# Graph attention in duos: one stretch of scores and one of contexts for two graphs

## The reference

```python
h = maximum(layernorm(x), 0)
q, k, v = heads(h @ Wq + bq), heads(h @ Wk + bk), heads(h @ Wv + bv)
scores = einsum('bhqd,bhkd->bhqk', q, k) / sqrt(64)
probs = softmax(scores + where(adj, 0, -9e15), axis=-1)
ctx = einsum('bhqk,bhkd->bhqd', probs, v)
out = x + (merge_heads(ctx) @ Wf + bf)
```

## Time and profile before

| what | value |
|---|---|
| median of three runs | 1001.98 us (1000.74 to 1003.02) |
| the profiled execution | 1000.85 us |
| its span in the trace | 999.0 us |
| granted TensorE clock, mean | 0.991 of full speed |

### The profile page before, as it was taken

One profiled execution on the slowest core, in us unless ns is written; L12 is line 12 of the kernel. 1 busy time (PEld: TensorE's weight loads), 2 busy tenths in 40 slices (PEclk: granted clock), 3 DMA queues, 4 the chain that ended last, 5 costly groups with the idle time before them and its releaser, 6 DMA issues.

```text
span 999.0 us, 28223 instructions
## 1 busy us (share of the span) xinstructions
PE 948.1 (95%) x8649; PEld 510.8 (51%) x8649; DVE 838.4 (84%) x1621; ACT 780.8 (78%) x2373; POOL 670.3 (67%) x1163
## 2 busy tenths in 40 slices
PE   1889999999999999999999999999999999999976
PEld 0445555555555555555555555555555555555543
DVE  4688888888888888898888888888889888888774
ACT  3687788888878888888888887888888888888663
POOL 4676677777776767767777677776776777777431
PEclk9999999999999999999999999999999999999997
DMA  7447656566566565655656656656565565666454
GB/s 199 75 90 152 123 126 141 127 139 147 130 135 136 129 140 130 148 133 126 141 127 141 145 130 133 138 129 139 132 148 133 124 143 128 140 146 121 92 94 90
DMA packets 359834, 130.86 MB, mean 131 GB/s; under 512 B 325376, under 2 KB 359808, under 8 KB 359808
## 3 DMA queue, kind: packets, MB, share of 16 engines
q1 hardware_dynamic: 359808, 130.54, 60.4%
HBM read 29.82 MB, written 25.17 MB: 55 GB/s over the span
## 4 chain that ended last, share of the span: by engine, by line
issue 44%; POOL 41%; PE 5%; ACT 2%; POOLq 2%; DVE 2%; DMA 2%; SPq 0%; DVEq 0%; ACTq 0%
POOL x_bias L807 13%; POOL s L816 11%; POOL rstd L775 7%; POOL mask L786 3%; POOL shift L778 2%; POOL rstd L770 2%; PE ps_qk L301 2%; POOL shift L772 2%; DMA pt<-parts 2%; POOL h_parts L795 1%; POOLq L165 1%; PE ps_v L301 1%; PE ps_r L301 1%; ACT s L473 1%; DVE s L650 1%
## 5 line engine op out<-in xcount | busy, mean ns | idle before, releaser
L473 ACT ACTIVATE s<-s,neg_max 128x128 f32<-128x128 f32 x768 | 297.7, 390 | 53.3 <-DVE neg_max L664 53.3
L816 POOL TENSOR_TENSOR s<-s,inv_sums 128x384 f32<-128x384 f32 x256 | 212.2, 829 | 132.7 <-DVE inv_sums L639 132.7
L795 POOL TENSOR_TENSOR h_parts<-h,h_parts 128x384 f16<-128x384 f32 x128 | 121.3, 948 | 146.1 <-ACT h_parts L515 146.1
L301 PE MATMUL ps_v<-w_hi_v,ht 128*128 128x384 f16 x768 | 209.4, 328 | 0.0
L301 PE MATMUL ps_qk<-ht,w_hi_q 128*128 128x512 f16 x576 | 172.5, 381 | 3.6 <-DVE w_lo_q L545 3.3
L301 PE MATMUL ps_qk<-ht,w_hi_k 128*128 128x512 f16 x576 | 171.3, 379 | 0.0
L807 POOL TENSOR_TENSOR x_bias<-x_in,out_bias 128x384 f32<-128x384 f32 x128 | 170.1, 1329 | 0.4
L494 ACT ACTIVATE parts<-s 128x768 f16<-128x768 f32 x128 | 107.3, 838 | 55.0 <-POOL s L816 55.0
L650 DVE SCALAR_TENSOR_TENSOR s<-ps_s,unscale,mask 128x384 f32<-128x384 f32 x256 | 145.2, 609 | 1.0
L473 ACT ACTIVATION_READ_ACCUMULATOR s<-s,neg_max 128x1 f32 x768 | 145.5, 189 | 0.0
L301 PE MATMUL ps_r<-w_hi_f,ct_hi 128*128 128x384 f16 x384 | 128.2, 334 | 14.3 <-DVE ct_lo L688 13.1
(11 more groups left out here) (77 smaller groups left out, 1806.6 us busy)
## 6 DMA issues: line engine op xcount, KB each, us to landing
x_in<-in_x SPq DMA_DIRECT2D x128, 192.0 KB, 2.9
out<-y SPq DMA_DIRECT2D x128, 192.0 KB, 2.1
ht<-h_parts SPq DMA_TRANSPOSE x128, 2.9
adj_in<-in_adj SPq DMA_DIRECT2D x32, 64.0 KB, 2.7
pt<-parts SPq DMA_TRANSPOSE x128, 3.7
w_raw_f<-in_L_gnn_Wf SPq DMA_DIRECT2D x1, 576.0 KB, 5.2
w_raw_q<-in_L_gnn_Wq SPq DMA_DIRECT2D x1, 576.0 KB, 6.2
w_raw_v<-in_L_gnn_Wv SPq DMA_DIRECT2D x1, 576.0 KB, 7.3
```

The source lines that it names most:

```text
L301: last = mm(psum, parts_a[a](i), parts_b[b](i), start=n == 0, stop=n == len(todo) - 1)
L473: last = activation(s[:, b, hd, :], s[:, b, hd, :], ACT.Exp, bias=neg_max[:, b, hd:hd + 1], accum_out=sums[:, b, hd:hd + 1])
L795: nc.gpsimd.tensor_tensor(h_parts[:, b, 1, :], h[:, b, :], h_parts[:, b, 0, :], ALU.subtract).then_inc(h_lo_ready, 1)
L816: nc.gpsimd.tensor_tensor(s[:, b, half, :], s[:, b, half, :], inv_sums[:, b, half].unsqueeze(2).to_broadcast([128, PAIRS, NODES]), ALU.mul ...
```

## The change

The unit of a slot becomes a duo, two graphs, 0 and 1. A slot of TensorE now has three tiles, the values of duo t+1, the projections of duo t-3, the scores of duo t and the contexts of duo t-2:

```diff
-                scores(t, k)
-                projection(t - 3)
-                qk_tile(tiles[0])
-                context(t - 2, k - 2)
-                v_tile()
-                if two:
-                    qk_tile(tiles[1])
+                qk_tile(0)
+                qk_tile(1)
+                projection(0)
+                values(0)
+                qk_tile(2)
+                values(1)
+                projection(1)
+                scores(0)
+                scores(1)
+                context(1)
+                context(0)
```

PSUM is divided anew: four banks for the scores of two graphs, two for tiles, and two that values, projections and contexts share (`ps_m`):

```diff
-        ps_s = ps("ps_s", [128, 2, 512])
+        ps_s = ps("ps_s", [128, 2, 2, 512])
         ps_qk = [ps(f"ps_qk{i}", [128, COLS]) for i in range(2)]
-        ps_c = ps("ps_c", [128, 512])
-        ps_r = ps("ps_r", [128, 512])
-        ps_v = [ps(f"ps_v{i}", [128, 512]) for i in range(2)]
+        ps_m = ps("ps_m", [128, 2, 512])
```

On the shared banks `projection(0)` and `values(0)` wait for the remainder of the contexts (`ct_lo_ready`), `values(1)` for `residual(0)` (`y_ready`), `projection(1)` for `lower_v(0)` (`v_ready`), `context(1)` for `lower_v(1)` and `context(0)` for `residual(1)`. The order of ScalarE in a slot becomes:

```diff
+                upper_context()
+                norm(0)
+                qk_upper(0)
+                upper_probs(1)
+                exponentials(0, 0)
+                qk_upper(1)
+                exponentials(0, 1)
+                v_upper(0)
+                exponentials(1, 0)
+                qk_upper(2)
+                v_upper(1)
+                upper_probs(0)
+                norm(1)
+                exponentials(1, 1)
+                upper_h()
```

That of VectorE:

```diff
+                masked_scores(0)
+                lower_context()
+                maxima(0)
+                qk_lower(0)
+                lower_probs(1)
+                masked_scores(1)
+                maxima(1)
+                residual(0)
+                qk_lower(1)
+                spread()
+                lower_v(0)
+                spread_done()
+                reciprocals(0)
+                mean_and_variance()
+                qk_lower(2)
+                lower_v(1)
+                residual(1)
+                lower_probs(0)
+                reciprocals(1)
```

And that of GpSimd:

```diff
                 factors()
-                mask_of_next()
+                normalised(1)
                 lower_h()
                 biased_x()
+                wait_for_mask()
                 normalised(0)
-                normalised(1)
+                mask_of()
```

Instructions that become wider: the masked scores, the reciprocals and `normalised` take all six heads of a graph at once; `lower_h`, `upper_h`, `biased_x`, `upper_context`, `lower_context`, the mask and the factors take both graphs of a duo at once. `lower_probs` keeps its 768 columns:

```diff
+                def lower_probs(i):
+                    u = t - (1, 2)[i]
...
+                    wait(dve, parts_hi, 2 * u + 1 + i)
+                    tt(parts[:, i, 1, :], s[:, i, :, :].rearrange("p h n -> p (h n)"), parts[:, i, 0, :],
                        ALU.subtract).then_inc(parts_lo, 1)
...
+                def masked_scores(i):
+                    u = t - 1
...
+                    wait(dve, scores_ps, 2 * u + 1 + i)
+                    wait(dve, mask_ready, u + 1)
+                    wait(dve, parts_lo, 2 * u - 1 + i)
...
                 def biased_x():
-                    u, r = t + XB, (k + XB) % RING
+                    u, r = t - 1, (k - 1) % RING
...
+                    wait(pool, xr_loaded[r], 4 * (u - r) + 16)
+                    nc.gpsimd.tensor_tensor(x_res[:, r, :, :], x_res[:, r, :, :],
+                                            out_bias[:, :].unsqueeze(1).to_broadcast([128, 2, FEAT]), ALU.add
                                             ).then_inc(xb_ready, 1)
```

x is loaded twice: once for the layer norm seven duos ahead (`x_in`, one DMA per graph), and again into `x_res` (one DMA per duo) for the residual sum. SyncE's order in a slot:

```diff
+                if valid(t + LOAD):
+                    u, r = t + LOAD, (k + LOAD) % RING
...
+                        wait(sp, parts_lo, 2 * t - 3)
+                    sp.dma_start(x_in[:, r, 0, :], x_rows[:, bass.ds(2 * u, 1), :].rearrange("n g f -> n (g f)")
...
+                    sp.dma_start_transpose(pt[:, k % 2, 0, :, :], parts[:, 0, :, :].rearrange("p a n -> p (a n)")
...
+                        wait(sp, h_lo_ready, t + TURN + 1)
+                    sp.dma_start(x_in[:, r, 1, :], x_rows[:, bass.ds(2 * u + 1, 1), :].rearrange("n g f -> n (g f)")
...
+                    sp.dma_start_transpose(ht[:, ((k + TURN) % RING) // 2, (k + TURN) % 2, :, :].rearrange("p a (g n) -> p (a g) n", g=2),
+                                           h_parts[:, b, :, :].rearrange("p a n -> p (a n)")).then_inc(h_turned[b], 16)
...
+                        wait(sp, parts_lo, 2 * t - 2)
+                    sp.dma_start(x_res[:, k, :, :], x_rows[:, bass.ds(2 * t, 2), :]).then_inc(xr_loaded[k], 16)
...
+                    sp.dma_start_transpose(pt[:, k % 2, 1, :, :], parts[:, 1, :, :].rearrange("p a n -> p (a n)")
...
+                        wait(sp, y_ready, 2 * u + 1 + i)
+                        sp.dma_start(out_rows[:, bass.ds(2 * u + i, 1), :].rearrange("n g f -> n (g f)"), y[:, i, :]
...
+                    sp.dma_start(adj_in[:, at, :, :], adj_rows[:, bass.ds(2 * t + GROUP, GROUP), :]
```

More of the change, by code:

```diff
@@ L174, in slots @@
                 for i in range(RING):
-                    slot(base + i, FIRST + i)
-            for t in range(LOOP_END, GRAPHS + LATE):
+                    slot(base + i, i)
+            for t in range(LOOP_END, DUOS + LATE):
                 slot(t, t % RING)
[L179 to L186, removed]
-        TILE = [(0, 0), (1, 0), (1, 1), (0, 1), (1, 2), (0, 2)]
[L191 to L199, removed]
+        TILE = [(0, 0), (1, 0), (1, 1), (0, 1), (1, 2), (0, 2)]
         x_rows = x.rearrange("g n f -> n g f")
@@ L323, in slot, with qk_tile @@
             def slot(t, k):
[L324 to L331, removed]
+                static = isinstance(t, int)
+                def qk_tile(i):
+                    if not valid(t + AHEAD):
+                        return
+                    tile = 3 * (k % 2) + i
+                    wn, pair = "qk"[TILE[tile][0]], TILE[tile][1]
+                    group, at = 1 - k // 2, slice(pair * 128, (pair + 1) * 128)
+                    if k % 2 == 0 and i == 0:
+                        for b in range(2):
+                            wait(pe, h_turned[b], 8 * (t + AHEAD) + 16)
+                    if static and t == -AHEAD and i < 2:
+                        wait(pe, w_lo_ready, 1 + i)
+                    wait(pe, qk_out, 3 * (t + AHEAD) + i - 1)
+                    split_product(ps_qk[(k + i) % 2].rearrange("p (d n) -> p d n", d=2),
+                                  [lambda i: w_hi[wn][:, i, at], lambda i: w_lo[wn][:, i, at]],
+                                  [lambda i: ht[:, group, :, i, :], lambda i: ht[:, group, :, KT + i, :]], (qk_ps, 1))
@@ L333, in scores @@
+                def scores(i):
                     if not valid(t):
                         return
[L335 to L338, removed]
+                    at = (k % 2) * 2 + i
+                    cols = slice(at * NODES, (at + 1) * NODES)
+                    wait(pe, masked, 2 * (t - 1) + 1 + i)
+                    if i == 0 and k % 2 == 0:
+                        wait(pe, qk_out, 3 * t + 6)
+                    if static and t == 0 and i == 0:
@@ L362, in qk_tile @@
-                def qk_tile(tile):
-                    if not project:
-                        return
-                    wn, pair = "qk"[TILE[tile][0]], TILE[tile][1]
-                    at = slice(pair * 128, (pair + 1) * 128)
-                    if start:
-                        wait(pe, w_lo_ready, 1 + 2 * tile)
-                    if j == 0 and tile == tiles[0]:
-                        for b in range(2):
-                            wait(pe, h_turned[b], 8 * (done + 2) + 16)
-                    wait(pe, qk_out, 2 * done - ((2 if tile == tiles[0] else 0) if two else 1))
-                    split_product(ps_qk[tile % 2][:, :],
-                                  [lambda i: w_hi[wn][:, i, at], lambda i: w_lo[wn][:, i, at]],
-                                  [lambda i: ht[:, 1 - p, i, :], lambda i: ht[:, 1 - p, KT + i, :]],
-                                  (qk_ps, 1 if two else 2))
@@ L432, in weights @@
             def weights(t):
[L433 removed]
+                if t == -3:
                     upper_weights()
             def slot(t, k):
[L437 to L454 removed]
@@ L657, in maxima @@
-                def maxima(t, k):
-                    if not valid(t):
+                    wait(dve, exp_done, 2 * u + 1 + i)
+                    nc.vector.reciprocal(inv_sums[:, i, :], sums[:, i, :]).then_inc(inv_ready, 1)
+                def masked_scores(i):
+                    u = t - 1
+                    if not valid(u):
+                        return
+                    wait(dve, scores_ps, 2 * u + 1 + i)
+                    wait(dve, mask_ready, u + 1)
+                    wait(dve, parts_lo, 2 * u - 1 + i)
+                    nc.vector.scalar_tensor_tensor(
+                        out=s[:, i, :, :], in0=ps_s[:, i, :, 0:PAIRS * NODES], scalar=unscale[:, 0:1],
+                        in1=mask[:, i:i + 1, :].to_broadcast([128, HEADS, NODES]),
+                        op0=ALU.mult, op1=ALU.add).then_inc(masked, 1)
```

587 lines of the change are left out of this document (271 added, 316 removed).

## The result

The changed kernel takes 1013.33 us (median of four runs, 1011.47 to 1016.84), the one before 1002.5 beside it: 1.0114 times the time, 95% interval 1.0082 to 1.0146. Slower was the forecast, with 1008 us. The profiled execution is the slowest of the four, 1016.84 us; its span is 1015.0, and the mean granted clock is 0.988.

The account below looks back on a forecast made before the run. TensorE bounds the kernel before; after the change a 14.96 us ring. First scores 51.9, slot 1 to 61.9, 56 slots to 899.7, four to 955.9, two to 976.3, tail to 1006.0, plus 1.85: 1008 us; 8-in-10 range 957 to 1042.

Parts of the forecast that it names:

- Each is ready 0.4 us or more ahead: Shared banks: `values(1)` waits for `residual(0)`, `context(1)` for `lower_v(1)`, `context(0)` for `residual(1)`; claimed to cost nothing.
- the ring: Chain of waits over VectorE, GpSimd and ScalarE from `exponentials(1, 1)` to the next duo's: 14.96 us per two graphs.
- The wait: VectorE's `lower_probs(1)` held until 0.14 us before GpSimd's `biased_x` ends: 1.1 us taken, 0.18 us the least.
- The floor of 14.05: TensorE's time per duo if nothing else binds: 13.75 us of products plus three boundaries, 0.30 us.
- the rival's 957 us: Way-is-free rival: `lower_probs(1)` gets in ahead of `biased_x` or hardly waits, ring under TensorE's floor, 957 us; chance 0.22.
- The ring of 13.85 without the wait: Same VectorE, GpSimd and ScalarE chain without the `biased_x` wait: 5.14 + 8.71 = 13.85 us, under TensorE's floor.
- the 1006.0 of the sum: Predicted span from first scores (51.9 us), the slots to last scores (976.3) and the tail: 1006.0 us.
- 22.6 + 7.1 = 29.7: Tail after the last scores: today's 22.6 us plus 7.1 for the duo's second graph and wider instructions.
- the 56 slots: Middle duos, set by the ring at 14.96 us each: 837.8 us, from 61.9 to 899.7.
- the next four: Slots after statistics and h work are over, bound by TensorE's 14.05 us each: up to 955.9 us.
- the two without tiles: Last two slots before the last scores, run at 10.2 us each: up to 976.3 us.
- The DMA share: Queue's busy share, lifted by the second x load (25.2 MB on 130.5 MB) from 60.4% to some 72%.

Follow-up runs that it names:

- the kernel with the way free: Changed kernel with GpSimd's `biased_x` moved behind its wait for the mask, after `lower_probs(1)`: 958.54 us, 0.9584 times before; second run 960.55 us, 0.9586.
- the changed kernel's second profile: The changed kernel unaltered, run again beside the variant that loads x a third time: 1012.7 us, median of four runs.

## Why the prediction was right, and where its sizes were off

**The mechanism.** Of the four signs that it named three came: short and long durations of `lower_probs` (0.96 and 1.95 to 2.12), the long ones beginning inside `biased_x`; a duo near 15.0; three boundaries of 0.09 to 0.10 us. The fourth, where TensorE waits, came in part: at `projection(1)` for `v_lo`, 0.58 us per duo, but at `values(1)` for `y` too, 0.41. "Each is ready 0.4 us or more ahead" was wrong for `residual(0)`: it hangs on the same late VectorE, ahead of `lower_v(0)`. The sum of 0.99 is the ring's, whichever bank it is taken at.

**The lock.** The wait was taken as whole (1.1 us), not as the 0.18 us seen; measured, 1.95 - 0.95 = 1.0 in the duo shown and 1.16 in three of four. The Trainium skill (SBUF - State Buffer, section Who interferes with whom) has the rule that the first to issue holds the way for its whole instruction. The traces now agree behind instructions of GpSimd of 1.82 us and 1.00 us and, with the order turned round, where GpSimd's own row grows from 1.00 to 1.72 us. The context remainder, one of whose inputs comes from PSUM, runs beside `lower_h` from 516.26 on, and neither is longer than predicted (0.95, 1.65).

**The ring.** 14.96 predicted, 15.02 measured. The wide instructions were sized right by fixed part and slope (1.47, 1.65, 1.82 for 1.47, 1.65, 1.81; the context remainder 0.95; masked scores 1.02 for 1.05). `biased_x` began 4.57 after the exponentials for 4.58, and `lower_probs(1)` 0.68 later, in most duos 0.52, for 0.56. Two hand-overs that I had counted as back to back cost 0.09 and 0.10: `masked_scores(1)` begins 0.13 after the end of `lower_probs(1)`, for which it waits (1.08 after VectorE went on, for 0.99), and `upper_probs(0)` 1.59 after the start of `normalised(0)` for 1.49. Of the other steps behind the wait most are as booked or a little shorter (the masked scores 1.06 for 1.09, `lower_v(0)` 0.46 for 0.50); together they give 0.13 back. So the 0.06 by which the ring was off is what two errors, 0.19 and 0.13, leave of each other.

**Without the wait.** The floor of 14.05 and the rival's 957 us were 14.03 and 958.5 to 960.6. The rival's condition (VectorE ahead of `biased_x`) was missed by 0.52 to 0.68 us; that it stood so near is why 957 had to lie inside the range. The ring of 13.85 without the wait shows in no run, since TensorE's floor covers it; 15.02 less the wait of 1.16 would make it 13.86.

**The ends: the term that was off.** Of the 9.0 us by which the span passed the 1006.0 of the sum, the start has 1.2 (first scores at 53.14 for 51.9), the slots up to the last scores 0.7 (978.23 for 976.3), and the tail the other 7.1: 36.8 us from the last scores, where 22.6 + 7.1 = 29.7 was put. That the slots came so near is in part luck: the 56 slots were 1.9 longer than the sum had them, the next four 0.4, and the two without tiles 1.5 shorter. The chain that ended last, in the changed kernel:

```profile
977.34 5.59 DMA pt<-parts
...
982.97 1.64 PE ps_m L380 x36
...
985.47 0.96 DVE ct_lo L660
...
988.28 1.03 DVE s L621
...
998.15 5.32 DMA pt<-parts
...
1003.52 1.71 PE ps_m L380 x36
...
1007.11 4.95 PE ps_m L272 x18
```

The sum let the last scores start the last chain. But TensorE, without tiles, does the last scores 7.24 us after those before, while VectorE's list still has the context remainder ahead of `masked_scores(1)`, and that waits for a transpose with nothing left to cover it. So the last masked scores begin 10.1 us after the last scores, in the kernel before 2.3 (978.73 in its chain, against 976.40); 3.7 of the 7.7 were counted. The other 3 us lie behind it. The two projections take 4.95 us, not 2 x 1.47: TensorE had waited 2.51 us for `pt`, its granted clock fell to 0.50, the lower of its two levels, soon after it went on, and 384 columns then take 0.32 us from start to start. The windows of the changed kernel show it (the clock is the third number from the end):

```profile
1004.00:1010.00 6.00, 4.10 (x36) 2.35 (x31) 0.96 (x1) 0.81 (x1) 0.00 (x0) 0.50 0.00 0
```

And the last transposes land in 5.32 us, 4.67 before.

But these 3 us belong to that execution, the slowest of its four. In the changed kernel's second profile (span 1010.5 us) the masked scores are as late, 10.0 us after the last scores, and the rest of the tail is not:

```profile
997.59 3.68 DMA pt<-parts
...
1004.41 3.11 PE ps_m L272 x18
```

```profile
1004.00:1010.40 6.40, 3.10 (x18) 1.68 (x18) 1.58 (x3) 0.00 (x0) 0.00 (x0) 1.00 0.17 61
```

Transposes, contexts and projections take 4.0 us less there, TensorE had waited 0.87 us for `pt`, and the tail is 32.8 us, 3.1 over the sum. So the step that was mis-sized in both is the way from the last scores to the last masked scores, 4.0 us more than counted; what follows was 0.9 less than counted in the second profile and 3.1 more in the first. In six of the nine profiles of the changed kernel and its variants the last two projections take 4.4 to 5.0 us, in three 3.1. That the longer wait brings the lower clock is argued from the first two, not tested.

**The DMA share** was put at 72% and is 67.3%. The bytes were right (155.70 MB), but 19% more bytes kept the queue busy for only 13% longer in all (share times span), and the span grew. In the kernel with the way free it is 71.8%, because that span is 5% shorter than the changed kernel's.

## What to carry to other kernels

When instructions of VectorE with two SBUF inputs share a stretch with GpSimd's, widening GpSimd's is not free even where GpSimd idles: work out, from one common event, which of the two starts first, and put the wide instruction that nobody waits for behind an event that follows the VectorE one. Look for the loss in durations (one operation, one shape, two lengths), not in the waits, and test an edit's worth only when the engine that it spares sets the period. Price the drain as a chain of its own, with transposes uncovered, not as the old tail plus what is wider, and give it a range: the same kernel's took 36.8 us in one execution and 32.8 in another, at different granted clocks.

## What the runs showed of the hardware that was not expected

GpSimd loses to the same VectorE instruction, in an instruction of two columns. The power for the layer norm (L735) takes 1.52 us in the changed kernel, where it starts together with `lower_probs(0)` at 512.81, and 0.70 with the way free (second run), where it starts 0.52 us ahead of it:

```profile
512.81 1.52 POOL L735 TENSOR_TENSOR rstd<-rstd,minus_half 128x2 f32<-128x2 f32 x1
```

```profile
512.67 0.70 POOL L735 TENSOR_TENSOR rstd<-rstd,minus_half 128x2 f32<-128x2 f32 x1
513.19 0.95 DVE L668 TENSOR_TENSOR parts<-s,parts 128x768 f16<-128x768 f32 x1
513.46 0.74 POOL L739 TENSOR_TENSOR shift<-shift,rstd 128x2 f32<-128x2 f32 x1
```

There the next one, `shift`, starts inside `lower_probs(0)` and takes 0.74 us for 0.19. So a small instruction waits for a wide one as long as a wide one would. It cost nothing in the changed kernel only because `normalised(1)` waits for the reciprocal anyway: `shift` ends at 514.60, `normalised(1)` begins at 514.83.
